# A listing begun in the wait for pair values, a sooner first scaling, another order of the last norms, and ten products of constants ahead of the first sequences

## The reference

```python
def _L0(x, agg, pairs, Wq, bq, Wk, bk):              # 10000 listed pairs (sub, obj)
    q = (x[sub] @ Wq.T + bq); k = (x[obj] @ Wk.T + bk)    # 8 heads
    att = (q * k).sum(-1) / sqrt(64)                 # per pair and head
    scores = zeros.at[:, sub, obj].set(att); scores = where(agg == 0, -inf, scores)
    scores = scores.at[:, di, di].set(1e-07)
    return softmax(scores).sum(heads) / 8 @ x
def _L1(x, adj, W_seq, a1, a2, W_out, b_out):        # 16 heads
    seq = x @ W_seq
    scores = leaky_relu(seq.a1[:, None] + seq.a2[None, :]) masked by adj
    return elu(softmax(scores) @ seq @ W_out + b_out)
x = layernorm(x + _L0(x, adj, ...)); x = layernorm(x + _L1(x, adj, ...))
```

## Time and profile before

| what | value |
|---|---|
| median of 3 runs | 415.32 us (413.97 to 416.71) |
| profiled execution | 415.14 us |
| its span | 413.4 us |
| PE busy | 362.1 us, 88% |
| DVE busy | 328.6 us, 79% |
| ACT busy | 205.9 us, 50% |
| POOL busy | 189.7 us, 46% |
| DMA | 65.11 MB, mean 157 GB/s |

### The profile page before, as it was taken

The page is one execution under the profiler, slowest core; times in us unless marked ns, Lnnn a source line. Parts: engine busy times, 40 slices in busy tenths (PEclk is TensorE's granted clock), DMA queues, the critical chain, the costliest instruction groups (busy, mean ns, idle before and its releaser), DMA issues.

```text
span 413.4 us, 5272 instructions
## 1 busy us (share of the span) xinstructions
PE 362.1 (88%) x1638; PEld 198.3 (48%) x1638; DVE 328.6 (79%) x868; ACT 205.9 (50%) x467; POOL 189.7 (46%) x212
## 2 busy tenths in 40 slices
PE   1599999999989898799988982779999999999990
PEld 1155555455344353588777861334444444444450
DVE  0999899876547996777778757689999999999754
ACT  3866756546423121455545431012465667776782
POOL 7777777777510000000000007887877777782000
PEclk9999999999999999899999995889999999999997
DMA  7999253355891330851111126656655767673113
GB/s 253 372 380 376 108 203 103 112 195 141 198 243 59 77 103 1 304 203 59 54 52 57 51 79 170 189 169 181 186 157 157 196 185 217 176 201 106 43 52 133
DMA packets 37063, 65.11 MB, mean 157 GB/s; under 512 B 17953, under 2 KB 19105, under 8 KB 34977
## 3 DMA queue, kind: packets, MB, share of 16 engines
q1 hardware_dynamic: 27936, 42.46, 31.0%
q0 software_dynamic: 9088, 22.20, 19.6%
HBM read 53.50 MB, written 8.52 MB: 150 GB/s over the span
## 4 chain that ended last, share of the span: by engine, by line
PE 46%; POOL 24%; DVE 14%; issue 10%; DMA 2%; ACT 2%; DVEq 0%; SPq 0%; POOLq 0%
POOL pr L504 20%; PE ps L915 16%; PE ps L799 13%; PE ps L832 12%; POOL adjT L593 3%; DVE arenaA L1287 2%; PE ps L788 2%; PE ps L823 2%; DMA adjT<-seqtab,eidx 1%; DMA pr<-in_adj_dram,aidx 1%; PE ps L626 1%; DVE arenaA L1283 1%; DVE arenaC L1719 1%; DVE stats L1725 1%; PE ps L780 1%
## 5 line engine op out<-in xcount | busy, mean ns | idle before, releaser
L593 POOL DMA_INDIRECT adjT<-seqtab,eidx x80 | 81.3, 1016 | 148.9 <-DMA seqtab<-scores 127.0
L626 PE MATMUL ps<-arenaB,adjT 128*128 128x512 f16 x512 | 117.9, 388 | 4.9 <-ACT adjT L975 3.1
L504 POOL DMA_INDIRECT pr<-in_adj_dram,aidx x79 | 81.8, 1035 | 24.0 <-issue 24.0
L915 PE MATMUL ps<-adjT,stage 128*128 128x512 f32 x160 | 79.9, 642 | 13.4 <-DVE adjT L1907 13.4
L626 PEld LDWEIGHTS ps<-arenaB,adjT 128*128 128x128 f16 x512 | 50.0, 100 | 64.9 <-DVE arenaB L1277 3.8
L799 PE MATMUL ps<-stage 128*128 128x272 f32 x256 | 63.0, 400 | 1.5 <-ACT stage L1061 1.5
L1907 DVE TENSOR_TENSOR adjT<-adjT 128x512 f32<-128x512 f32 x80 | 53.8, 734 | 2.2 <-ACT adjT L1187 2.2
L832 PE MATMUL ps<-adjT 128*128 128x512 f32 x120 | 54.0, 592 | 0.0
L799 PEld LDWEIGHTS ps<-stage 128*128 128x128 f32 x256 | 48.4, 194 | 11.3 <-ACT stage L1061 2.1
L915 PEld LDWEIGHTS ps<-adjT,stage 128*128 128x128 f32 x160 | 28.6, 200 | 48.6 <-issue 45.7
L1287 DVE MAX8 arenaA<-arenaA 128x8 f16<-128x256 f16 x120 | 40.7, 411 | 0.5
(11 more groups left out here) (267 smaller groups left out, 492.5 us busy)
## 6 DMA issues: line engine op xcount, KB each, us to landing
stage<-in_adj_dram SPq DMA_DIRECT2D x16, 1024.0 KB
arenaA<-in_x_dram SPq DMA_DIRECT2D x4, 1024.0 KB, 13.3
seqtab<-arenaA SPq DMA_DIRECT2D x16, 256.0 KB, 2.0
out_dram<-arenaC SPq DMA_DIRECT2D x16, 256.0 KB, 3.2
arenaB<-in_x_dram SPq DMA_DIRECT2D x1, 1536.0 KB, 10.7
adjT<-seqtab,eidx POOLq DMA_INDIRECT x80, 3.8
pr<-in_adj_dram,aidx POOLq DMA_INDIRECT x79
arenaC<-in_L_gnn_Wq_dram SPq DMA_DIRECT2D x1, 1024.0 KB, 9.4
```

The lines of the kernel that those rows point to most:

```text
L504: g.indirect_dma_start(out=avals[:, t:t + 1], out_offset=None, in_=adj_flat, in_offset=bass.IndirectOffsetOnAxis(ap=aidx[:, t:t + 1], axis ...
L593: g.indirect_dma_start(out=G[:, b % GR, k, :], out_offset=None, in_=seqtab, in_offset=bass.IndirectOffsetOnAxis(ap=eidx[:, b * KE + k:b * ...
L626: ins = t.matmul(bank(4 + b % 2), adjT[:, b, j, :], xsplit[:, w, j, :], start=(j == 0 and w == 0), stop=(j == NB - 1 and w == 1))
L915: t.matmul(bank(2 + b % 2), ehot[:, b % 2, k, :], G[:, b % GR, k, 0:D], start=False, stop=(k == KE - 1), skip_group_check=True)
```

## The change

Four things are done, in one edit.

1. `listing` is cut in two, `list_keys` (mask, diagonal, first 4 MAX) and `list_top` (the rest). `list_keys(13)` now stands ahead of `count_pairs`, `list_top(13)` behind `fetch_pairs`; listing 13 is gone from `last_rows`.
2. On PE the steps for the pairs stand one quarter of a block later than before (one more quarter of `multiply` ahead of each), `pe_sum_flags` stands ahead of `pair_scatter` and not behind the branch. ACT's first scaling waits for `fast_done` and not for `pairs_ready`; PE waits for `fast_done` ahead of `correct(0)` and for `pairs_ready` only ahead of `correct(2)`.
3. `keep_busy` is new: 4 products of two constant tiles ahead of `turn_x1(0)` and 6 ahead of `make_seq(0)`, into a bank that nobody reads.
4. At the end the norms of blocks 12 and 13 stand ahead of `add_elu(14)`, those of 14 and 15 behind everything; ACT's roots and parts are reordered to suit.

```diff
@@ PE @@
-                if b == 11:
-                    pair_offsets()
                 multiply(b, Q, 2 * Q)
...
+                if b == 11:
+                    pair_offsets()
+                multiply(b, 2 * Q, 3 * Q)
                 if b == 11:
                     pair_list()
...
+                if b == 14:
+                    count_rows()
+                multiply(b, 3 * Q, NB)
                 if b == 12:
                     pair_qk()
                 if b == 14:
-                    count_rows()
                     pair_sums()
-                multiply(b, 3 * Q, NB)
...
             multiply(NB - 1, 0, Q)
+            multiply(NB - 1, Q, 2 * Q)
+            pe_sum_flags()
             pair_scatter()
-            multiply(NB - 1, Q, 3 * Q)
+            multiply(NB - 1, 2 * Q, 3 * Q)
...
             def correct(b):
-                if b == 0:
-                    pe.wait_ge(pairs_ready, 1)
                 pe.wait_ge(scaled, b + 1)
...
+            def keep_busy(n):
+
+                for _ in range(n):
+                    t.matmul(bank(2), identh[:], iota[:, 0:512], start=True, stop=True)
...
                 pe.wait_ge(flag_made, 1)
+                keep_busy(4)
                 turn_x1(0)
                 correct(1)
                 pe.wait_ge(l1_load, 16 * KT)
-                pe.wait_ge(wa_made, 2)
+                pe.wait_ge(pairs_ready, 1)
                 correct(2)
+                keep_busy(6)
                 make_seq(0)
...
             with pe.If(count < FEWER + 1):
-                pe_sum_flags()
+                pe.wait_ge(fast_done, 1)
                 correct(0)
@@ ACT @@
-                act.wait_ge(pairs_ready, 1)
+                act.wait_ge(fast_done if last_waits else pairs_ready, 1)
...
                     last_roots(LAST, LAST + 1, LAST // 2)
-                    norm_of(LAST - 2)
-                    elu_part(NB - 2)
                     act.wait_ge(var_made, NB + 2)
                     last_roots(LAST + 1, LAST + 2, LAST // 2 + 1)
-                    elu_half(0)
+                    elu_part(NB - 2)
+                    norm_of(LAST - 2)
+                    for c in range(2):
+                        elu_half(c)
                     act.wait_ge(var_made, NB + 3)
                     last_roots(LAST + 2, LAST + 3, LAST // 2 + 2)
-                    elu_half(1)
                     norm_of(LAST - 1)
@@ DVE @@
+            list_keys(NB - 3)
             count_pairs()
             place_pairs()
             fetch_pairs()
+            list_top(NB - 3)
 
             def last_rows():
-                listing(NB - 3)
                 listing(NB - 2)
...
                 finish(NB - 1)
-                for b in range(LAST + 1, NB - 1):
-                    add_elu(b, late)
-                    last_norm(b - 1, LAST // 2 + b - LAST)
-                add_half(0, late)
+                add_elu(LAST + 1, late)
+                for b in (LAST, LAST + 1):
+                    last_norm(b, LAST // 2 + b - LAST + 1)
+                add_elu(LAST + 2, late)
+                for c in range(2):
+                    add_half(c, late)
+                v.bn_aggr(mv[:, NB - 1, :], stats[:, NB - 2:NB, :]).then_inc(var_made, 1)
                 last_norm(NB - 2, LAST // 2 + NB - 1 - LAST)
-                add_half(1, late)
-                v.bn_aggr(mv[:, NB - 1, :], stats[:, NB - 2:NB, :]).then_inc(var_made, 1)
                 last_norm(NB - 1, LAST // 2 + NB - LAST)
```

More of the change, by code:

```diff
@@ L687, in pair_scatter, with pe_sum_flags @@
                          stop=True).then_inc(scat_made, 1)
+            def pe_sum_flags():
+                pe.wait_ge(bad_made, 1)
+                t.matmul(ps[:, 3, 64:65], ones[:], bad[:, 3:4], start=True, stop=True).then_inc(bad_summed, 1)
             def count_rows():
@@ L709, in _ @@
                     pair_rows()
-                multiply(b, 2 * Q, 3 * Q)
+                if b == 14:
+                    count_rows()
+                multiply(b, 3 * Q, NB)
                 if b == 12:
@@ L863, in pe_dense @@
                         ins.then_inc(L_pe.sem, 1)
-            def pe_sum_flags():
-                pe.wait_ge(bad_made, 1)
-                t.matmul(ps[:, 3, 64:65], ones[:], bad[:, 3:4], start=True, stop=True).then_inc(bad_summed, 1)
             def open_bank(k):
                 t.matmul(bank(k), identh[:], iota[:, 0:512], start=True, stop=True).then_inc(opened, 1)
+            def keep_busy(n):
+                for _ in range(n):
+                    t.matmul(bank(2), identh[:], iota[:, 0:512], start=True, stop=True)
             def pe_first_norm():
                 pe.wait_ge(flag_made, 1)
+                keep_busy(4)
                 turn_x1(0)
@@ L1260, in _ @@
             links, sp_args = [0], [0]
+            SEG = N // 8
             def link(ins):
@@ L1277, in low, with list_keys @@
                 v.tensor_tensor(xsplit[:, 1, b, :], x_in[:, b, :], xsplit[:, 0, b, :], ALU.subtract).then_inc(low_done, 1)
-            def listing(b, key=key, top=top, junk=junk, offdiag=offdiag):
-                seg = N // 8
+            def list_keys(b, key=key, top=top, offdiag=offdiag):
                 dve.wait_ge(row_cast, b + 1)
@@ L1285, in listing, with list_top @@
                 link(v.tensor_tensor(own, own, offdiag, ALU.mult))
-                for k in range(8):
-                    ins = v.max(top[:, 0, 8 * k:8 * k + 8], key[:, k * seg:(k + 1) * seg])
+                for k in range(4):
+                    v.max(top[:, 0, 8 * k:8 * k + 8], key[:, k * SEG:(k + 1) * SEG])
+            def list_top(b, key=key, top=top, junk=junk):
+                for k in range(4, 8):
+                    ins = v.max(top[:, 0, 8 * k:8 * k + 8], key[:, k * SEG:(k + 1) * SEG])
                 link(ins)
@@ L1294, in listing @@
                                        ALU.mult, ALU.add, deg[:, 1, b:b + 1]).then_inc(row_listed, 1)
+            def listing(b):
+                list_keys(b)
+                list_top(b)
             def score_weights(step):
@@ L1440, in _ @@
             link(v.tensor_scalar(offdiag0, identh[:], -1.0, 1.0, ALU.mult, ALU.add))
-            listing(0, key0, top0, junk0, offdiag0)
+            list_keys(0, key0, top0, offdiag0)
+            list_top(0, key0, top0, junk0)
             for b in range(4, NB):
```

## The result

The changed kernel takes **408.71 us** (median of 6 runs, 407.80 to 410.82) beside 414.33 us (6 runs, 412.22 to 416.71) of the kernel before. The ratio is 0.9878, 95% interval 0.9852 to 0.9904: 5.6 us of the median, so 1.0 to 1.5% less time. The profiled execution took 409.74 us with a span of 407.9; the kernel before had 415.14 and 413.4, so the span is 5.5 shorter. The forecast was 409.6.

The account below looks back on a forecast made before the run. The chain of waits was PE 46%, POOL 24%, DVE 14%, with DVE carrying most of the pair stage. Gains of 2.0 + 1.4 + 1.3 + 0.9 = 5.6 us from 415.14 gave 409.5, stated as 409.6 us; range 407.4 to 412.3.

Parts of the forecast that it names:

- Listing 13: DVE around the pair count: half the listing fills the 3.15 us idle; attend starts 2.00 us sooner, capped by PE's pair_qk.
- The keys, put at nothing: DVE ahead of the pair count: list_keys takes 2.89 us in a gap of 3.15, so it costs nothing.
- The wait behind the branch: DVE behind its branch: an unexplained 7.17 us, expected to stay the same behind the later branch.
- Rival 5: The wait behind DVE's branch doubles to 14.34 us, giving a slower 415.8 us; chance 0.04.
- Scaling on `fast_done`: ACT's first scaling starts at 158.8, not 162.21: 1.4 us gained beyond the listing's 2.0.
- Rival 3: The first scaling waits for something else, x rows or bank: 411.0 us; chance 0.05.
- Ten constant products: PE's idles ahead of first turn and first sequences: products fit free, clock stays at 2.4 GHz; 1.3 us gained.
- The turn of block 2: PE's turn would come 0.22 us late behind DVE's rows, giving back some of the 1.48 us clock gain.
- Rival 1: PE's clock falls all the same at the first sequences: 410.9 us; chance 0.14.
- The end: Last norms on DVE: the last norm comes 0.9 us sooner; the store may leave as little as 0, 0.9 taken.
- The sum: Whole kernel: 2.0 + 1.4 + 1.3 + 0.9 = 5.6 us gained; stages between only move.
- Rival 4: The clock's fall at 274 to 279 us goes away or comes elsewhere, worth 1.7: 407.9 us; chance 0.12.

Follow-up runs that it names:

- listing back: Changed kernel with listing 13 whole and back behind DVE's branch; 409.69 us, ratio 0.9893.
- products alone: Kernel before with the ten constant products and nothing else of the change; 412.74 us, ratio 0.9945.
- second profile of the same kernel: Changed kernel run again without any edit, beside two further kernels; 409.46 us, ratio 0.9866.
- one body: Changed kernel with DVE's last_rows once, ahead of its branch, and only the many-pairs work inside the branch; 410.99 us, ratio 0.9918.
- without the products: Changed kernel without its ten constant products; 411.48 us, ratio 0.9935.
- the end as before: Changed kernel with the order of the last norms, roots and parts on DVE and ACT as in the kernel before; 409.20 us, ratio 0.9874.
- doubled: Changed kernel with 8 and 12 constant products instead of 4 and 6; 411.06 us, ratio 0.9929.
- late loads: Changed kernel with the first three loads of W_seq issued behind the transposition of block 15; 408.12 us, ratio 0.9852.
- old PE order: Changed kernel with PE's order of the pair steps and all waits for the first scaling as in the kernel before; 411.26 us, ratio 0.9933.
- profiles with the twelve products: Changed kernel with 12 more constant products ahead of block 2 of the second layer, 409.41 us; with late loads as well, 407.55 us.

## Why the prediction was right

- **Listing 13: forecast 2.00, measured 1.57.** The mechanism held: the keys went into the 3.15, DVE came out early and `pair_qk` capped it. The term was mis-sized by 0.43: 0.32 for the gather of the nodes, which I took as fixed and which landed at 125.76, and 0.11 for the handover from PE to DVE. `attend` follows 9.7 to 9.8 behind that landing whenever DVE is early. Set against this, the three profiles with the whole listing behind the branch have `attend` 1.9 (before), 1.0 (listing back) and 0.9 us (products alone) later than the gather asks. So the term is 1 to 2 us, as the gather falls.
- **The keys, put at nothing, cost something in the profiled execution.** In the seven profiles where the count still waits for the values, it starts 2.45 to 2.89 us behind the end of POOL's last gather of them. In the changed kernel's that gather ended at 109.41, 0.9 sooner than before (110.32); by my estimate from these two numbers the values were there at 111.9 to 112.3, and DVE, which had its keys to finish first, counted at 113.03. In the second profile of the same kernel it still waited 0.29 for the values. So the gap holds the keys with nothing to spare, and they cost between nothing and about 1 us.
- **The wait behind the branch: taken as 7.17, measured 6.14** (6.12 in the second profile of the same kernel). It is the jump's, as the one body shows, and its length goes with the transfers: 2.84, 3.47 and 6.14 at 2, 124 and 230 GB/s. The error had no price, since `attend` waited for PE. Rival 5 asked for 14.3; the longest seen is 7.41. I had written that no row shows a fetch, and that nothing in the profile says what the 7.17 us are; the profile's transfers by queue do, with one packet of code in each of these waits. What grows with the transfers is the time until it starts. That the wait shrank when its start moved 2.2 us back fits: the loads began at 118.6 to 118.8 in both kernels, so a later jump meets less of them (waits of 6.32 to 7.41 in the three profiles with the branch near 119, 5.46 to 6.14 in the seven with it near 121.5 and the same loads). Why it is 7.17 and 7.41 in two of those three and 6.32 in the third stays open.
- **Scaling on `fast_done`: forecast 1.4, measured 1.43**, and 1.42 from the other side, with PE's order put back. Rival 3 is out: `scale_x` has the weights as its last releaser.
- **Ten constant products: forecast 1.3, measured 1.47**, 1.7 when taken out and 1.5 when put in alone. The turn of block 2, for which I took off 0.22, came 0.05 behind DVE's rows (170.23 + 0.55 to 170.83); the second sequences start 5.06 behind the first, where before it was 6.53, so it gave nothing back. I had forecast idles of 0.35 and 0.16; they are 0.30 and 0.16. Rival 1 went by the Trainium skill, "TensorE: Matmul & The Clock Gate", section "A second HAM failure mode: psum-queue depth-cycling"; here the granted clock stayed 1.00 through both short idles, so the case doesn't show that fall. It shows that two idles of 1.26 and 1.52 with nothing else in the stretch end in it (before, and without the products), and that idles of 0.30 and 0.16 with the ten products in it do not. So the length of an idle alone does not decide: with the products, the clock also lived through the 2.07 of the one body. I had put it down to more work in the stretch, and that fits all of these; the idles need not be filled to the brim.
- **The end: forecast 0.9, measured 0.88.** That is at the last norm. The span ended 5.5 earlier while the last norm came 5.62 earlier, so the store took back about 0.1 in this execution; in the second profile of the same kernel it took 0.9, all of it, and some 0.4 in the mean (see the end as before). I had named this and then counted the whole 0.9, so here the forecast had luck.
- **The sum: forecast 5.6; the profiled executions differ by 5.4** (415.14 and 409.74), the medians by 5.6. The mechanisms of the four terms held, but that the sum fits to 0.2 is in part luck: the listing gave 0.43 less, the clock 0.17 more, and 0.27 came from steps that I had put at nothing (0.07 between the first scaling and the first sequences, 0.20 in the second layer). The second profile of the changed kernel has a span of 409.2, 1.3 longer: 0.1 of this up to the second sequences, 0.4 in the second layer, 0.8 in the stores.
- **Rival 4**, at 0.12, was no gain that waits to be had: the clock fell again in block 2, and in other kernels it falls in block 1 (last section).

## What to carry to other kernels

Price a part by the time at which the next late thing comes, and then ask what that thing's own spread is: here a gather decides whether two microseconds are two or one. Idles of TensorE just ahead of a long run of fp32 products are worth some products of constants, up to the idle's length and not beyond; measure the idle first. Behind a jump, look in the profile's transfers for a packet of the instruction queue: here the engine went on 2 us after it began, and it began later the more other transfers were under way. So move loads that nobody is waiting for out of a jump's way. And give the last step the stores' spread: a norm that ends 0.9 sooner may end the kernel 0 to 0.9 sooner.

## What the runs showed that I had not expected

- In each of the eleven profiles without filling products there, the granted clock falls in exactly one of two blocks of the second layer: block 1's ten products or block 2's take 6.23 us, and 4.53 in the other. With the fall in block 2 (before, changed twice, without products, doubled, one body, late loads) 220.5 to 221.1 us pass from the second sequences to the last 24 products; with it in block 1 (listing back, old PE order, old end, products alone) 219.4 to 220.0. That is 0.5 to 1.7 us that go to no edit, and with products of constants ahead of block 2 it is 219.55 to 219.61, no better than a fall in block 1. This fits that those twelve don't show in a median; which block it was in the executions that were not profiled isn't known.
- The rows suggest why it is one and not both. Ahead of block 1 PE idled 2.65 to 3.02 us in the four profiles where the clock fell there, and 2.17 to 2.53 in the seven where it did not. Ahead of block 2 it then idled 1.19 to 1.50 in the four, as the slow block 1 had used up the time, and 2.80 to 3.17 in the seven. No run tested it, and one of the profiles with the twelve products has 2.65 ahead of block 1 and no fall.
- A wait behind a jump shrinks from 6.14 to 3.47 when 106 GB/s of loads move out of its way, with no other edit, and a single 8 KB packet of code is what it waits for.
